# Rotary step of a fused attention kernel: the sine product taken in place on VectorE, the halves crossed in two additions on GpSimd

## The reference, cut to what matters

```python
q = l2norm(q) * qs
k = l2norm(k) * ksc
q = q * cos * scale + rotate_half(q) * sin * scale
k = k * cos * inv + rotate_half(k) * sin * inv      # rotate_half(x) = [-x2, x1]
out = local_attention(q, k, v)                       # softmax over 64 keys per query
```

## Time and profile before

| | |
|---|---|
| median of 3 runs | 3241.17 us (3239.01 to 3252.73) |
| the profiled execution's own time | 3247.59 us |
| its span, first to last instruction | 3245.8 us |
| mean granted TensorE clock over the span | 0.988 |
| PE, DVE, ACT, POOL busy | 3132.2, 2712.8, 2522.3, 2442.1 us |

### The profile page before, as it was taken

The page is one execution under the profiler, slowest core; times in us unless marked ns, Lnnn a source line. Parts: engine busy times, 40 slices in busy tenths (PEclk is TensorE's granted clock), DMA queues, the critical chain, the costliest instruction groups (busy, mean ns, idle before and its releaser), DMA issues. The chain is left out here.

```text
span 3245.8 us, 151130 instructions
## 1 busy us (share of the span) xinstructions
PE 3132.2 (97%) x63141; PEld 2614.1 (81%) x63141; DVE 2712.8 (84%) x6367; ACT 2522.3 (78%) x5220; POOL 2442.1 (75%) x1536
## 2 busy tenths in 40 slices
PE   7869999999999999999999999999999999999996
PEld 6757888888888888888888888888888888888885
DVE  6559888888888888888888888888888888888883
ACT  3337888887888888888888888888888888788884
POOL 6458787787777777777777778777777777777773
PEclk9889999999999999999999999999999999999998
DMA  4551111132111122211122211122111122121111
GB/s 168 195 189 47 45 44 46 46 88 72 50 43 45 50 81 63 63 42 47 50 81 63 63 45 44 47 79 70 57 50 44 45 79 72 56 57 45 47 54 29
DMA packets 109237, 211.00 MB, mean 65 GB/s; under 512 B 19344, under 2 KB 40080, under 8 KB 104592
## 3 DMA queue, kind: packets, MB, share of 16 engines
q1 hardware_dynamic: 106544, 193.36, 20.2%
q10 hardware_dynamic: 2016, 7.98, 0.7%
HBM read 46.91 MB, written 28.53 MB: 23 GB/s over the span
## 5 line engine op out<-in xcount | busy, mean ns | idle before, releaser
L456 POOL TENSOR_TENSOR qks<-work 128x1024 f32<-128x1024 f32 x384 | 910.2, 2370 | 524.9 <-DVE work L1216 508.1
L843 PE MATMUL psum<-wparts,xhi 128*128 128x512 f32 x2304 | 788.6, 423 | 14.9 <-POOL xlo L442 8.0
L464 POOL TENSOR_TENSOR qkr<-qks,rnorm 128x1024 f32<-128x1024 f32 x384 | 731.5, 1905 | 0.4
L605 ACT ACTIVATE sq<-psum 128x512 f32<-128x512 f32 x768 | 455.3, 593 | 117.8 <-PE psum L843 90.0
L1214 DVE TENSOR_TENSOR work<-psum,rot 128x512 f32<-128x512 f32 x768 | 523.6, 682 | 6.1 <-ACT sq L605 3.7
L1187 DVE TENSOR_REDUCE ssq<-sq 128x8 f32<-128x512 f32 x768 | 475.9, 657 | 0.0
L843 PE MATMUL psum<-wparts,xlo 128*128 128x512 f32 x1152 | 454.5, 395 | 0.0
L927 PEld LDWEIGHTS psum<-probT,vsh 64*64 64x64 f32 x12288 | 326.2, 134 | 140.6 <-issue 140.2
L843 PEld LDWEIGHTS psum<-wparts,xhi 128*128 128x128 f32 x2304 | 380.1, 191 | 60.7 <-issue 7.7
L868 PE MATMUL psum<-kT,qTs 64*32 64x64 f32 x24576 | 421.5, 218 | 0.0
L868 PEld LDWEIGHTS psum<-kT,qTs 64*32 64x32 f32 x24576 | 359.6, 107 | 64.7 <-issue 64.0
(11 more groups left out here) (151 smaller groups left out, 6137.5 us busy)
## 6 DMA issues: line engine op xcount, KB each, us to landing
vsh<-vtok SPq DMA_DIRECT2D x384, 192.0 KB, 2.4
vsh<-vtok SPq DMA_DIRECT2D x384, 64.0 KB, 2.7
wsplit<-wstage SPq DMA_DIRECT2D x15, 1024.0 KB, 6.4
wparts<-wsplit SPq DMA_DIRECT2D x30, 512.0 KB, 4.1
xsh<-xs_in SPq DMA_DIRECT2D x192, 64.0 KB, 2.4
ff_x<-x_mid SPq DMA_DIRECT2D x96, 128.0 KB, 2.4
wraw<-Wqkv_dram SPq DMA_DIRECT2D x18, 512.0 KB, 4.1
wsplit<-wstage SPq DMA_DIRECT2D x5, 1066.0 KB, 8.1
```

The lines of the kernel that those rows point to most:

```text
L456: pool.tensor_tensor(qks[:, :, :], rcos, rsin, ALU.add).then_inc(s["add_ready"], 1)
L464: pool.tensor_tensor(qkr[:, n % 2, :, :], qks[:, :, :], rnorm[:, :].unsqueeze(2).to_broadcast([P, 2 * OCT, DH]), ALU.mult).then_inc(s["qkr ...
L605: act.activation(sq[:, w * OCT:(w + 1) * OCT, :], bank[w].rearrange("p (h n) -> p h n", n=DH), ACT.Square).then_inc(s[("sqq_ready", "sqk_r ...
L843: mm = pe.matmul(out, xparts[xp][:, ti, :], wparts[:, SECTION_AT[w, oc], wp_, :], start=(k == 0), stop=(k == 2))
```

## The change

The sine product on VectorE now reads the bank in place, 512 columns in one instruction, into `rsin` without a swap. The swap is done by the addition on GpSimd: it becomes two instructions of 16 x 32 columns each, the first half of every head from the first half of `rcos` and the second of `rsin`, and the other way round. The table is stored at the source column: its two halves and their signs are exchanged on the host, and its gains are no longer swapped. `rotq_ready`, `rotk_ready` and `add_ready` stay on the last instruction of their part.

```diff
                 need(pool, "qkr_ready", n)
-                pool.tensor_tensor(qks[:, :, :], rcos, rsin, ALU.add).then_inc(s["add_ready"], 1)
+                H = DH // 2
+                pool.tensor_tensor(qks[:, :, 0:H], rcos[:, :, 0:H], rsin[:, :, H:DH], ALU.add)
+                pool.tensor_tensor(qks[:, :, H:DH], rcos[:, :, H:DH], rsin[:, :, 0:H], ALU.add).then_inc(s["add_ready"], 1)
...
                 dve.tensor_tensor(rc, x3, table(0, 0, DH), ALU.mult)
-                dve.tensor_tensor(rs[:, :, 0:H], x3[:, :, H:DH], table(1, 0, H), ALU.mult)
-                dve.tensor_tensor(rs[:, :, H:DH], x3[:, :, 0:H], table(1, H, H), ALU.mult).then_inc(s[("rotq_ready", "rotk_ready")[w]], 1)
+                dve.tensor_tensor(rs, x3, table(1, 0, DH), ALU.mult).then_inc(s[("rotq_ready", "rotk_ready")[w]], 1)
...
-        tab[:, 1, n, :] = np.concatenate([-sin * m, sin * m], -1)
+        tab[:, 1, n, :] = np.concatenate([sin * m, -sin * m], -1)
...
-    swapped = _np.concatenate([gain[..., DH // 2:], gain[..., :DH // 2]], -1)
...
-        "gains": _np.stack([gain, swapped], 1).reshape(1, -1),
+        "gains": _np.stack([gain, gain], 1).reshape(1, -1),
```

More of the change, by code:

```diff
@@ L1200, in rotation @@
                     return
-                H = DH // 2
                 ti, layer = n // UPT % TPB, n // UNITS
```

## The result

| | before | after |
|---|---|---|
| median of 20 runs each | 3247.44 us (3239.01 to 3252.73) | 3241.18 us (3236.40 to 3248.46) |
| the profiled execution | 3247.59 us, span 3245.8 | 3240.91 us, span 3239.1 |

The ratio is 0.9983, 95% interval 0.9976 to 0.9990. That is a small but real gain of about 6 us, within the 0.5% that the forecast called no change. The forecast of 3241 us is met to the microsecond by chance: it was "no change", put at the median of the three runs of before then shown, and over 20 runs that kernel's median is 6.3 us higher. So what has to be explained is a gain of 6 us where none was forecast.

What follows compares the result with a forecast made beforehand. PE's own instructions were taken as the bound. Loop 0, fill -0.7 to 0 and end up to +0.13 us summed to 0 within 1 us, so 3241 us, the median of the runs shown; range 3234 to 3257.

Steps and rivals of the forecast that it cites:

- no change: Whole kernel: the time stays within about 0.5%, 16 us; chance 0.88, own range 3235 to 3254 us.
- PE's list is the bound: Loop: PE's own instructions set the pace, 97% busy, shortest step 5.80 us; the change touches none of them.
- The prices: Rotation on VectorE 1.20 us, 0.06 less; GpSimd's pair of additions 2.46 us, 0.13 more a unit.
- Loop: 0 from its waits: Term for PE's waits in the loop: the change neither adds to them nor shortens them, 0 us.
- The same 30 us of waits: Expected sign in the profile after: PE's loop waits stay at 30 us, none for `qkr` or `work`.
- Half rows dear on GpSimd: Rival at L457 and L458: runs of 32 cost extra starts, giving 3280 us or 3494 us; chance 0.08.
- Its point of 3.5 us a pair: Half-rows rival: in the fast steps GpSimd's slack is gone once the pair of additions takes 3.5 us.
- Its price of 39 us: Half-rows rival: a 3.69 us pair lacks 0.2 us in about half of 384 steps, 39 us.
- POOL cheaper by the crossed addresses: Rival on GpSimd's additions: the pair at 2.1 us, still 3241 us; counted as part of the no-change case.
- VectorE as the bound: Rival: VectorE's savings come through, 3195 us or 3126 by lengths; shares chance 0.04 with unseen PE relief.
- some relief of PE over 16 us that I don't see: Unplaced faster case: PE gains over 16 us; shares chance 0.04 with VectorE as the bound.
- the likeliest case: Whole kernel: no change, chance 0.88, with 3241 us predicted.

Runs made afterwards that it cites:

- `gpsimd_alone`: The kernel before, with GpSimd's addition as two instructions of 16 x 32 columns, each from the same halves; 3249.06 us, 1.0008 of before.
- `no_sine`: The changed kernel without the sine product on VectorE, which is left out of the result; 3221.69 us, 0.9923 of before.

## Why the prediction was right, and which step of it was wrong

**PE's list is the bound: right.** Its step of 5.80 us and its 97% did not move, and neither 118 us of busy time less on VectorE's rotations nor 73 us more on GpSimd's additions came through.

**The prices: right.** The rotation 1.20 us by starts as charged; the pair 2.48 against 2.46. VectorE's busy time is 49 us less in all, near the 46 by starts; the forecast had expected some 115 less there, which was wrong, since busy time counts overlapping records once and the 118 us are the sum of lengths. GpSimd's is 58 us more (65 expected).

**"Loop: 0 from its waits": wrong.** The rows say that 23.9 of PE's 30 us of waits are for Gelu, and I took that for ScalarE's own affair. "The same 30 us of waits" were expected after; 18.5 of them are left for Gelu and about 25 in all. I asked only whether PE waits for the rotation (0.2 us) or for `qkr` (none), not who holds the one it does wait for. The row names the last link. Followed back, Gelu hangs on a run of ScalarE work that starts with VectorE's `sdiff`, and that on two rotations. The term should have been -48 x 2 x 0.06 = -5.8 us, all from the trace of the kernel before; it measured 5.4 us in the waits and 6.3 us in the medians. It lies below the 0.5% that I called no change, so the class, the range and the likeliest case held.

**Half rows dear on GpSimd: did not happen.** No run shows halves one and a half times as dear, as its 3.69 us had them; a half took 1272 ns with gaps and 1276 without. Its point of 3.5 us a pair agrees with the estimate of 3.4. Its price of 39 us for 3.69 us of additions was less than half of the 94 measured. I had counted the fast steps alone and left out the loop through `work`, for which VectorE waits 281.8 us there; that this is the reason is likely, but not shown.

**POOL cheaper by the crossed addresses: no.** A half takes 1278 and 1283 ns crossed, 1272 (median) uncrossed in `gpsimd_alone`.

**VectorE as the bound: no.** Without the sine product 460 us of VectorE were worth 20 us. The other half of that chance, "some relief of PE over 16 us that I don't see", is what happened in kind, but at 6 us.

**The version that beats both** is the reordered one: with Gelu ahead of the turned keys 3209.38 us for the changed kernel, and with the mask moved too 3209.42 and 3210.99 us for the changed and the old one, 1.1% under before. With both reorderings, the rotation no longer makes a difference that shows.

## What to carry to other kernels

When one engine is the bound, list its few remaining waits and follow each back through the engine that it names, over instructions that run without a pause, to the last idle time; a saving on that stretch counted here until something else ended the wait, though its engine was idle 1.0 us a step on average (0.12 us a block counted in full, and of the 1.20 us freed by `no_sine` only 0.25, from 2.66 to 2.41). A mean idle time was here an upper bound of slack and no more: VectorE with 1.0 us a step could not hide 0.66, GpSimd with 1.67 could not hide 1.36 (2.33 to 3.69). And before an instruction is made cheaper, look whether it can be moved off the stretch: here a different order gave the old kernel 37 us, the cheaper rotation 6.

## What the runs showed of the hardware

- A wait cost PE time without idle time in its row. In the block at 1560 us the release came late, the weight load started 0.03 us ahead of its matmul instead of 0.16, and over the blocks the next interval was 0.33 us instead of 0.23 (medians). The waits of PEld show it (12.9 us for Gelu in the reordered old kernel, 7.3 in the changed one, none with the mask moved too).
- Two ACT table loads of 1.28 us each (L694 and L700, 48 each, all 1283 ns) stand around each Gelu, and in the block shown the Gelu started 0.02 us behind the first (1516.70 + 1.28 to 1518.00). The load started 0.02 us behind the end of the instruction ahead of it (1516.07 + 0.61 to 1516.70).
- On VectorE two products of 256 columns in runs of 32 take 0.66 us by starts, one of 512 columns 0.60. So one instruction fewer was worth 0.06 us; no run prices the runs of 32 on VectorE by themselves.
